# The queries' channel swap in the preparation stage of a fused two-layer language-model tower: from a permutation matmul to on-chip transfers

## The reference, cut to what matters

```
xqk = x @ wq                                  # x: 4 x 512 x 192, 12 heads of 64 channels
XQ = causal_dwconv(xqk, conv_q_w, conv_q_b)   # out = b + sum over k < 4 of w[k] * x shifted by 4-k
XK = causal_dwconv(xqk, conv_k_w, conv_k_b)
XV = x @ wv
def rope(x, cos, sin):                        # neighbouring channels form a pair
    x1, x2 = even channels, odd channels
    return pairs (x1 * cos - x2 * sin, x1 * sin + x2 * cos)
XQ, XK = rope(XQ, cos, sin), rope(XK, cos, sin)
ttt_lr = sigmoid(x @ lr_w.T + lr_b)
...                                           # the recurrence over 32 steps of 16 tokens
```

## Time and profile before

| | us |
|---|---|
| runs of the kernel, three | 1373.02, 1375.83, 1375.84 (median 1375.83) |
| the profiled execution's own time | 1372.88 |
| its span | 1371.1 |
| its mean granted TensorE clock | 0.963 |
| busy over the span: PE, DVE, ACT, POOL | 1252.3, 912.3, 729.3, 381.5 |
| preparation stage, first projection to the next stage's first matmul | 373.5 to 557.9 |

### The profile page before, as it was taken

One profiled execution on the slowest core, in us unless ns is written; L12 is line 12 of the kernel. 1 busy time (PEld: TensorE's weight loads), 2 busy tenths in 40 slices (PEclk: granted clock), 3 DMA queues, 4 the chain that ended last, 5 costly groups with the idle time before them and its releaser, 6 DMA issues. The chain is left out here.

```text
span 1371.1 us, 29272 instructions
## 1 busy us (share of the span) xinstructions
PE 1252.3 (91%) x11347; PEld 862.8 (63%) x11347; DVE 912.3 (67%) x2294; ACT 729.3 (53%) x1529; POOL 381.5 (28%) x445
## 2 busy tenths in 40 slices
PE   4889999799779999899999998899986899899998
PEld 3532333345647777677777776777864445588888
DVE  6588888413578777799888877888874899400001
ACT  1446555432224443688888884788874334443310
POOL 6500000100057777456666660000000344200000
PEclk9889999979989999999999999999998999999999
DMA  3342121300024234634343452122102300177811
GB/s 99 106 124 70 47 61 34 72 15 1 21 74 124 82 117 128 204 111 124 109 132 98 140 137 64 41 64 59 47 1 93 129 1 1 39 274 276 281 69 46
DMA packets 99287, 127.42 MB, mean 93 GB/s; under 512 B 24590, under 2 KB 87805, under 8 KB 94957
## 3 DMA queue, kind: packets, MB, share of 16 engines
q1 hardware_dynamic: 96556, 123.44, 29.5%
q0 software_dynamic: 1536, 1.59, 0.5%
q10 hardware_dynamic: 1056, 0.52, 0.1%
HBM read 89.06 MB, written 37.88 MB: 93 GB/s over the span
## 5 line engine op out<-in xcount | busy, mean ns | idle before, releaser
L1792 POOL TENSOR_SCALAR r_grD<-gr 32x192 f32<-32x192 f32 x192 | 101.8, 530 | 93.8 <-DVE gr L1686 45.9
L700 ACT ACTIVATE PT<-bank 128x1024 f32<-128x1024 f32 x96 | 94.3, 1023 | 59.5 <-PE bank L580 58.8
L641 DVE TENSOR_REDUCE mx<-bank 128x1 f32<-128x512 f32 x176 | 110.0, 682 | 12.2 <-PE bank L563 11.9
L1523 PE MATMUL bank<-r_grD,ek 128*128 128x256 f32 x384 | 100.0, 396 | 0.0
L2554 DVE TENSOR_TENSOR eo_all<-bank,m_b2s 128x768 f32<-128x768 f32 x8 | 7.7, 958 | 138.5 <-PE bank L2515 138.5
L2546 ACT ACTIVATE x_g<-bank,m_b1s 128x128 f32<-128x128 f32 x192 | 51.4, 399 | 75.7 <-PE bank L2497 75.7
L1523 PEld LDWEIGHTS bank<-r_grD,ek 128*128 128x128 f32 x384 | 67.7, 189 | 9.3
L2428 POOL TENSOR_SCALAR m_xs<-m_xs 128x256 f32<-128x256 f32 x4 | 2.5, 632 | 247.6 <-DVE m_xs L2319 247.6
L1736 ACT ACTIVATE r_t<-r_xh,r_cd 128x64 f32<-128x64 f32 x192 | 70.2, 429 | 0.8
L1514 PEld LDWEIGHTS bank<-gr,r_A 128*128 128x128 f32 x384 | 47.6, 190 | 33.7 <-DVE gr L1686 32.6
L1352 POOL TENSOR_TENSOR rope_c<-cy,p_rope 128x512 f32<-128x512 f32 x48 | 60.0, 1270 | 20.0 <-DVE cy L1205 20.0
(11 more groups left out here) (380 smaller groups left out, 3235.3 us busy)
## 6 DMA issues: line engine op xcount, KB each, us to landing
wb<-in_m_w SPq DMA_DIRECT2D x32, 1152.0 KB, 5.6
ek<-k_d SPq DMA_DIRECT2D x32, 384.0 KB
k_d<-t_late SPq DMA_DIRECT2D x46, 256.0 KB, 2.8
tgt<-c_d SPq DMA_DIRECT2D x33, 196.0 KB
c_d<-t_late SPq DMA_DIRECT2D x32, 196.0 KB, 2.9
g_d<-gr SPq DMA_DIRECT2D x32, 192.0 KB
o_G<-g_d SPq DMA_DIRECT2D x32, 192.0 KB, 3.0
qk_d<-a_parts SPq DMA_DIRECT2D x24, 192.0 KB, 3.0
```

What stands on the lines that cost most here:

```text
L641: v.tensor_reduce(mx[u % 2][:, j // 4, j % 4:j % 4 + 1], slot(f"A{u}.{j}"), AX.X, ALU.max).then_inc(*dve.did(f"max{u}.{j}"))
L700: a.activation(PT[kt % 2][:, 2 * hp:2 * hp + 2, :], STB[s % 2][:, :, :], ACT.Exp, scale=DH ** -0.5)\
L1523: last = t_.matmul(SP_[g][:, i * B * E1:(i + 1) * B * E1], ek[r][:, p, :], grD[g][:, i, :, :].rearrange("p b e -> p (b e)"), start=False, ...
L1792: last = g_.tensor_scalar(grD[g][rr, :, b, :], b3(gr[j % RING][rr, cols(g)]), 0.0, None, ALU.bypass)
```

## The change

The queries' permutation matmul r0 goes. In its place SP copies `cy` to `rope_s` with two transfers, one that reads the odd partitions and writes the even ones, and one the other way. Each moves 64 rows of 2 KB. DVE then multiplies `rope_s` in place by the sine table, so that both inputs of this multiplication are in SBUF. The keys stay as they were. Three hand-written lists change their order as well:

- DVE runs s0.n-1 after all taps of unit n, not between c10.n and c21.n.
- POOL runs z0.n-1 after m1.n and m0.n, not before them.
- SP issues the swap of unit m, then `k_d` of unit m-2 (and `c_d`). ACT's y.n+1 waits for the arrival of swap n-1 in place of r0.n-1.

The core of the diff (a semaphore list and the closing waits are left out):

```diff
@@ lists
         dve = Steps(sem("p_dve"), [s for n in range(B * HP + 1) for s in
                                    ([f"c11.{n}"] if n in U else []) + ([f"s1.{n - 1}"] if n else [])
-                                   + ([f"c10.{n}"] if n in U else []) + ([f"s0.{n - 1}"] if n else [])
-                                   + ([f"c21.{n}", f"c20.{n}", f"c31.{n}", f"c30.{n}"] if n in U else [])])
+                                   + ([f"c10.{n}", f"c21.{n}", f"c20.{n}", f"c31.{n}", f"c30.{n}"] if n in U else [])
+                                   + ([f"s0.{n - 1}"] if n else [])])
...
@@ SP
-                for n in U:
+                def swap(w, n):
+                    sp.wait_ge(*dve.at(f"c3{w}.{n}"))
+                    if n >= 2:
+                        sp.wait_ge(*pool.at(f"z{w}.{n - 2}"))
+                    for a in range(2):
+                        sp.dma_start(r2[a:P:2, n % 2, w, :], y[1 - a:P:2, n % 2, w, :]).then_inc(swapped[w][n % 2], 16)
+
+                for m in range(len(U) + 2):
+                    if m in U:
+                        for w in reversed(SWAPS):
+                            swap(w, m)
+                    if m < 2:
+                        continue
+                    n = m - 2
@@ PE
-                        for w in (1, 0):
-                            t_.wait_ge(*dve.at(f"c3{w}.{n}"))
-                            if n:
-                                t_.wait_ge(*dve.at(f"s{w}.{n - 1}"))
-                            t_.matmul(ROT[w], pair[:, :], y[:, n % 2, w, :], start=True, stop=True).then_inc(*pe.did(f"r{w}.{n}"))
+                        t_.wait_ge(*dve.at(f"c31.{n}"))
+                        if n:
+                            t_.wait_ge(*dve.at(f"s1.{n - 1}"))
+                        t_.matmul(ROT[1], pair[:, :], y[:, n % 2, 1, :], start=True, stop=True).then_inc(*pe.did(f"r1.{n}"))
@@ DVE
                 def partner(w, n):
+                    if w in SWAPS:
+                        v.wait_ge(*arrived(w, n))
+                        v.tensor_tensor(r2[:, n % 2, w, :], r2[:, n % 2, w, :], rope[:, 1, :], ALU.mult).then_inc(*dve.did(f"s{w}.{n}"))
+                        return
@@ ACT
-                                a.wait_ge(*pe.at(f"r{w}.{n - 1}"))
+                                a.wait_ge(*(arrived(w, n - 1) if w in SWAPS else pe.at(f"r{w}.{n - 1}")))
@@ POOL
                 for n in range(len(U) + 1):
                     if n:
-                        for w in (1, 0):
-                            rotated(w, n - 1)
+                        rotated(1, n - 1)
                     if n in U:
...
+                    if n:
+                        rotated(0, n - 1)
```

More of the change, by code:

```diff
@@ L1076, in ttt_prepare @@
         kst, (c_first, c_rest) = M["k_st"], M["c_st"]
+        swapped = [[sem(f"p_swap{w}{r}") for r in range(2)] for w in range(2)]
         U = range(B * HP)
         END = len(U) - 1
+        SWAPS = (0,)
+        arrived = lambda w, n: (swapped[w][n % 2], 32 * (n // 2 + 1))
         q_of, p_of = (lambda n: n // HP), (lambda n: n % HP)
@@ L1090, in ttt_prepare @@
                    + ([f"lr.{rate_of(n)}"] if n % HP == 3 else [])
-                   + ([f"r1.{n}", f"r0.{n}"] if n in U else [])])
+                   + ([f"r1.{n}"] if n in U else [])])
         pool = Steps(sem("p_pool"), [s for n in range(B * HP + 1) for s in
-                     ([f"z1.{n - 1}", f"z0.{n - 1}"] if n else []) + ([f"m1.{n}", f"m0.{n}"] if n in U else [])])
+                     ([f"z1.{n - 1}"] if n else []) + ([f"m1.{n}", f"m0.{n}"] if n in U else []) + ([f"z0.{n - 1}"] if n else [])])
         of = lambda b: slice(b * N, (b + 1) * N)
@@ L1122, in _ @@
                 sp.wait_ge(kept, 16)
+                for w in SWAPS:
+                    for r in range(2):
+                        sp.wait_ge(*arrived(w, END - 1 + r))
             @block.tensor
@@ L1214, in _ @@
                 for n in range(len(U) + 1):
-                    for w in (1, 0):
[L1216 to L1219, removed]
-                    if n in U:
+                    if n in U:
+                        tap(1, 1, n)
+                    if n:
+                        partner(1, n - 1)
+                    if n in U:
+                        tap(1, 0, n)
                         for k in (2, 3):
@@ L1223, in _ @@
                                 tap(k, w, n)
+                    if n:
+                        partner(0, n - 1)
                     if n == 0:
```

## The result

| | us |
|---|---|
| before, median of 4 runs | 1374.42 (1371.59 to 1375.84) |
| after, median of 4 runs | 1357.75 (1356.44 to 1361.78) |
| ratio | 0.9867, 95% interval 0.984 to 0.9895 |
| the profiled execution of after, and its span | 1361.78, 1360.0 |

The forecast was 1355.4 with a range of 1351.5 to 1366. The change gains 16.7 us by the medians, whose quotient is 0.988; the ratio in the table is the one on record, with its interval.

The account below looks back on a forecast made before the run. PE was taken to set the period, 6.55 us in plain units and 8.34 in long ones. Gains of 17.2 + 1.8 + 0 = 19.0 us took the middle, 1374.4, to 1355.4, range 1351.5 to 1366.

Parts of the forecast that it names:

- PE's 17.2 us: 20 units without r0's 0.86 us on PE; plain units take 5.69 us, long ones 7.48.
- s0's wait for m1: On DVE, s0 with two SBUF inputs waits 0.42 us for POOL's m1, bounds 0 and 0.75; DVE needs 5.57.
- My price for a need above 5.69: If DVE needs 5.90 us, the 16 plain units lose 16 x (5.90 - 5.69) = 3.4 us of the gain.
- the rival of the full wait: s0 waits to m1's very end, 0.75 us; DVE needs 5.90 and sets plain units: 1358.8 us, chance 0.20.
- m0 behind s0: On POOL, m0 meets s0 and loses at most 0.36 us; POOL needs 5.4 in 5.69 and is no bound.
- The port ring: POOL starts m0 before DVE gets in, so s0 waits for both, 1.67 us: 1373.5 us; chance 0.17 with mixtures.
- The transfer: Swap takes 3.4 us from issue to landing; it may land up to 5.0 us after c30, so cost 0.
- the late transfer: Slower rival: ACT's y waits for a swap as slow as 8.7 us, time 1385.4 us; chance 0.09.
- The formula for lateness: With ACT's y waiting for the swap, the period is (L + 6.4)/2; it decides above L = 5.0.
- SP and `c_d`: Behind `c_d` on SP's queue the swap lands at about 8.9 us after s1, just inside 9.0; cost 0.
- Start: In the second unit, half of r1 with r0's 3.57 us at half clock goes: 1.8 us, between 0 and 2.4.
- End: The last T waits for z1 on POOL, which does z0 ahead of it; gain 0, at most 1.46 us.

Follow-up runs that it names:

- c: The changed kernel without the swap's transfers; s0 reads a PSUM bank that one matmul fills in the first unit: 1359.12 us, ratio 0.9858 to before.
- d: The changed kernel with the sine table copied once to PSUM, so s0 has one input in each memory: 1361.73 us, ratio 0.989 to before.
- e: The changed kernel with SP writing 768 KB of SBUF to DRAM ahead of each swap, to make it late: 1376.03 us, ratio 0.9957 to before.
- g: The changed kernel with keys also swapped by transfer, s1 and s0 behind the taps, sine table in PSUM: 1351.49 us, ratio 0.9771 to before.
- a: The changed kernel's new order on DVE and POOL, but with matmul r0 kept and no transfers: 1374.69 us, ratio 0.9984 to before.
- h: The changed kernel with z1 of the last unit ahead of z0 of the unit before on POOL: 1366.18 us, ratio 0.9885 to before.
- b: The changed kernel's transfers with the old order on DVE and POOL, s0 between c10 and c21: 1377.70 us, ratio 1.0005 to before.
- f: The changed kernel with keys also swapped by transfer, s1 and s0 behind the taps, sine table in SBUF: 1379.04 us, ratio 0.9989 to before.

## Why the prediction was right, step by step

- **PE's 17.2 us: right.** 17.1 measured. It came out through other units than told: DVE needs more than 5.69 (below), so plain units take 5.78, and DVE falls behind PE by 0.09 in each of five and makes it good in the long unit, where it would otherwise wait (7.03 = 7.48 - 5 x 0.09). The short wait for PE before s1 in plain units, which the prediction named as a sign of being right, did not appear. `c` and `d`, where PE sets each unit, come to the same six units.
- **s0's wait for m1: the size was off.** I took 0.42 between 0 and 0.75, from the nearest row. It is 1.32 - 0.68 = 0.64: m1 ended at about 457.85 + 1.25 = 459.10, 0.75 after s0 was due, so it gave way only 0.1 before its end and not 0.33. The row was of a POOL operation of half the length. Records that follow each other on DVE overlap by 0.08 as well (s0 ends at 458.35 + 1.32 = 459.67, the next begins at 459.59), so 0.64 can hardly be told from a wait to the end. The page "SBUF — State Buffer" of the Trainium skill, section "Who interferes with whom", calls the port pair that VectorE and GpSimd share an exclusive lock. By that the wait is the whole overlap, 0.75; the measurement is nearer to that than to mine. With 0.64 DVE's need is 5.15 + 0.64 = 5.79, which is the period seen. My price for a need above 5.69 (16 times the excess) was wrong too: it would take 16 x 0.09 = 1.4, and the 20 units take 121.11 where 16 x 5.69 + 4 x 7.48 makes 120.96, so 0.15 is taken. The long units wait for PE by more than the excess of five plain ones. By this the rival of the full wait would have cost less than the 3.4 given, as five times 0.21 is 1.05 of the 1.79 that a long unit has to give; no run shows that case. So two errors, a wait taken too small and a price for it taken too high, left the sum where it was: that part of the hit is luck.
- **m0 behind s0: above the bound.** At most 0.36 was predicted, 0.45 measured (2.95 - 2.50), since s0 itself ended later. POOL needs some 5.5 and waited for DVE, not DVE for it. The port ring didn't close: s0 went in before m0 in all 20 units, and took 1.33 us at most.
- **The transfer: right, and with room.** 2.6 us to landing in place of 3.4; cost 0 by `c`. ACT's y waited for it in three plain units, which the prediction named as a sign of the late transfer; those swaps landed 4.3 to 4.4 us after c30, still inside its budget of 5.0, and no period grew. The formula for lateness held roughly in `e`.
- **SP and `c_d`: right in the sum, and thinner than told.** The prediction put the swap there at 4.9 us after c30, inside 5.0. It landed at 4.5, 5.3 and 6.0. ACT's wait for `c_d` grew from 4.9 to 10.2 us there, and the long units took it, as told. `g`, which has no slack there, shows what it costs without that cover.
- **Start: 1.8 predicted, 1.2 measured, and most of it has another cause.** From the first projection to s1 of the third unit it is 26.33 us in place of 27.55. But `a`, which keeps r0, has 26.50. So 1.05 comes from the new order, which lets r1 of the second unit start 0.6 earlier; the prediction had that only in its upper bound. Taking r0 away adds 0.17. These are PE's rows there in `a`, then in the changed kernel:

```profile
392.38 3.78 PE L1203 MATMUL bank<-cy,pair 128*128 128x512 f32 x4 [3.85 <-DVE cy L1224]
395.95 2.53 PE L1150 MATMUL bank<-t_xT,p_wq 96*128 96x512 f32 x4
```

```profile
395.31 2.08 PE L1202 MATMUL bank<-cy,pair 128*128 128x512 f32 x2 [3.79 <-DVE cy L1223]
397.18 3.62 PE L1150 MATMUL bank<-t_xT,p_wq 96*128 96x512 f32 x4
```

  The swap is 1.7 us shorter, but the projection behind it takes 1.1 more: the granted clock is still 0.50 (1.2 GHz) from 397.20 to 400.60 in the changed kernel, where it averaged 0.74 from 396.00 to 398.40 in `a`. The target's first matmuls lose most of the rest. This is the prediction's own caveat, that the clock may rise no earlier, and it took nearly all of the 1.8. That the term came out near its size is luck.
- **End: 0 predicted, 0.4 lost.** The prediction's "last s1" (539.27) is that of the last but one unit; here it is 526.36. The last T begins 9.32 after it (before 8.91), and waits for POOL as told. I had z1 done 8.7 after s1; z1 took 1.74, since the last s0 fell beside it (the swap of the last unit lands there). `h` shows the order z0 before z1 as the cause of 1.7: z0's 1.26 and the 0.45 by which z1 was longer. In `d`, without the conflict, the last T begins 8.4 after that s1. From T to the next stage it is 9.85, 0.2 more.

Together 17.1 + 1.2 - 0.4 - 0.2 = 17.7, the stage's difference. The main term, 17.1 of it, came by the mechanism that was forecast; the rest of the agreement is in part luck, as said. Open are the 5.4 us before the stage in the profiled execution, and why three of the swaps land later than the others.

## What to carry to other kernels

Before an operation moves off the bounding engine, work out the need of each other engine with the operands in their new place, and compare it over the whole cycle of short and long units, not unit by unit: here an excess in the short ones was free, since the long ones had waits to give. Before a gain is put down to a part that went, run the new order with that part kept (`a`): it had most of the gain at the start. A transfer in place of a matmul paid here only with its reader moved to where the data are due anyhow; the old place lost everything here (`b`). Where DVE and POOL work side by side, keep a constant operand of DVE in a PSUM bank that has come free: the same change lost its gain with the table in SBUF (`f`) and gave 2.3% with it in PSUM (`g`).

## What the runs showed of the hardware that I had not expected

- A DVE multiplication of 128x512 with both inputs in SBUF that comes up while POOL runs one of the same size waits until about 0.1 us before that one ends, and POOL's next one then waits for DVE (2.95 in place of 2.50 for two). With one input in PSUM neither waits (`d`, `g`).
- The conflict is a chain: two such DVE operations beside POOL's pair cost 1.73 us a unit (`f`), against 0.64 for one.
- The transfer that reads every second partition of SBUF and writes the others takes 2.1 us for 128 KB and 2.5 for 256 KB from issue to landing (`g`), so twice the size adds 0.4. These are medians: in the changed kernel single halves between 409 and 525 us took 1.9 to 4.2. The page "DMA: Bandwidth & Descriptors" of the Trainium skill, section "Anatomy of one DMA — SWDGE (gpsimd) path", gives a fixed 2.0 us and bytes / 436e3 on top, for transfers issued from GpSimd, which would be 2.3 and 2.6 as an estimate. The transfers here are issued by SP, and their medians come out 0.1 to 0.2 below that.
